# Two attention layers over 128 rows: a new order of the first layer's mixes, gated sum, turns and statistics

## The reference

```python
# layer 0: 8 heads of 32 channels, attention over the 256 tokens of a row
x = layernorm(x1d)                                  # over channels
q, k, v = split(x @ qkv_w.T)
aff = einsum('bmich,bmjch->bmijh', q, k)
gate = sigmoid(x @ gate_w.T + gate_b)
weights = softmax(aff + bias[:, None])              # bias = x2d @ x2d_w.T / sqrt(32)
out = (einsum('bmrch,bmirh->bmich', v, weights) * gate) @ final_w.T + final_b
# layer 1: 4 heads of 64 channels, |i - j| <= 16, no gate
```

## Time and profile before

| what | value |
|---|---|
| median of three runs | 3649.43 us |
| the profiled execution | 3664.15 us |
| its span, first to last instruction | 3662.3 us |
| mean granted clock of TensorE over the span | 0.969 of full speed |
| busy: PE, DVE, ACT, POOL | 92%, 82%, 76%, 59% |
| from 300 to 2200 us (layer 0): PE, DVE, ACT, POOL busy in 1900 us | 1788.69, 1685.45, 1680.21, 1496.18 us |
| granted clock from 300 to 2200 us | 1.00 |
| from 2400 to 3600 us (layer 1): PE, DVE, ACT, POOL busy in 1200 us | 1200.00, 969.89, 839.27, 493.42 us |

### The profile page before, as it was taken

The page is one execution under the profiler, slowest core; times in us unless marked ns, Lnnn a source line. Parts: engine busy times, 40 slices in busy tenths (PEclk is TensorE's granted clock), DMA queues, the critical chain, the costliest instruction groups (busy, mean ns, idle before and its releaser), DMA issues.

```text
span 3662.3 us, 122873 instructions
## 1 busy us (share of the span) xinstructions
PE 3372.3 (92%) x36747; PEld 3007.4 (82%) x36747; DVE 3002.9 (82%) x10850; ACT 2776.3 (76%) x8999; POOL 2177.9 (59%) x4107
## 2 busy tenths in 40 slices
PE   4459999999999999999999999799999999999999
PEld 1148888888888888888888888699999999999998
DVE  4458988888888888888888888688888888888887
ACT  1148888988888888888888988567667677776776
POOL 0047777777777777787777777444444444444443
PEclk7569999999999999999999999899999999999999
DMA  9921111111111111111111111011111111111111
GB/s 341 349 100 54 46 49 51 44 52 45 50 52 43 52 46 48 52 43 52 46 48 50 44 52 44 30 53 52 52 52 52 52 53 54 53 52 52 52 52 47
DMA packets 189032, 238.42 MB, mean 65 GB/s; under 512 B 11824, under 2 KB 176176, under 8 KB 184752
## 3 DMA queue, kind: packets, MB, share of 16 engines
q1 hardware_dynamic: 184368, 204.17, 17.7%
q10 hardware_dynamic: 4608, 33.56, 2.5%
HBM read 170.57 MB, written 67.11 MB: 65 GB/s over the span
## 4 chain that ended last, share of the span: by engine, by line
PE 58%; ACT 14%; issue 11%; DMA 6%; DVE 6%; POOL 2%; DVEq 1%; SPq 1%; ACTq 1%; POOLq 0%
PE work L477 24%; ACT prob L722 7%; PE work L486 7%; PE turn L527 5%; PE score L617 5%; PE mix L650 4%; DMA x_chunk<-xT 4%; PE mix L539 3%; PE score L505 3%; DMA x_tok<-x_nat 3%; PE turn L634 3%; ACT xnT L741 2%; ACT probT L728 2%; PE turn L635 2%; PE turn L636 2%
## 5 line engine op out<-in xcount | busy, mean ns | idle before, releaser
L364 POOL TENSOR_SCALAR prob<-prob,row_inv 128x256 f32<-128x256 f32 x2048 | 1068.0, 540 | 206.1 <-DVE row_inv L932 204.9
L722 ACT ACTIVATE prob<-prob,row_min 128x256 f32<-128x256 f32 x2048 | 1028.1, 507 | 128.3 <-DVE row_min L926 123.6
L477 PE MATMUL work<-src,w 128*128 128x256 f32 x7680 | 1067.5, 288 | 10.4 <-DVE src L915 6.7
L477 PEld LDWEIGHTS work<-src,w 128*128 128x128 f32 x7680 | 951.0, 189 | 12.3 <-DVE src L915 7.4
L415 POOL TENSOR_SCALAR prob<-prob,row_inv 128x160 f32<-128x160 f32 x1024 | 391.0, 401 | 767.4 <-DVE row_inv L1042 767.4
L926 DVE CUSTOM_DVE_ANT_0 prob<-score,neg_bias 128x256 f32<-128x256 f32 x2048 | 749.5, 417 | 17.2 <-PE score L505 10.1
L527 PE MATMUL turn<-ident,prob 128*128 128x128 f32 x3072 | 484.8, 280 | 120.0 <-ACT probT L728 101.4
L789 ACT ACTIVATE prob<-prob,row_min 128x160 f32<-128x160 f32 x1024 | 431.4, 426 | 141.7 <-DVE row_min L1035 141.6
L527 PEld LDWEIGHTS turn<-ident,prob 128*128 128x128 f32 x3072 | 336.3, 141 | 233.2 <-ACT probT L728 125.6
L477 PE MATMUL work<-att,wf 128*128 128x256 f32 x3072 | 432.1, 290 | 4.4 <-DVE att L981 3.0
L486 PE MATMUL work<-w,src 128*128 128x256 f32 x3072 | 425.8, 288 | 0.0
(11 more groups left out here) (110 smaller groups left out, 6225.7 us busy)
## 6 DMA issues: line engine op xcount, KB each, us to landing
pair_chunk<-pairT ACTq DMA_DIRECT2D x32, 1024.0 KB, 8.0
x_chunk<-xT SPq DMA_DIRECT2D x32, 1024.0 KB, 8.5
x_tok<-x_nat SPq DMA_DIRECT2D x128, 256.0 KB, 3.3
x_sb<-xT SPq DMA_DIRECT2D x128, 256.0 KB, 3.4
x1T<-y_sb SPq DMA_DIRECT2D x128, 256.0 KB, 2.2
x_sb<-x1T SPq DMA_DIRECT2D x128, 256.0 KB, 2.9
outT<-y_sb SPq DMA_DIRECT2D x128, 256.0 KB, 2.2
prob<-w_d SPq DMA_DIRECT2D x1, 1024.0 KB, 8.2
```

The lines of the kernel that those rows point to most:

```text
L364: pool.tensor_scalar(prob[:, h, ib], prob[:, h, ib], row_inv[:, h, ib:ib + 1], 1.0, ALU.mult, ALU.mult).then_inc(norm_done[0], 1)
L477: ins = pe.matmul(out[:, cb], w[:, of_w, kb, cols + cb * P:cols + (cb + 1) * P], x[:, of_x, kb], start=n == 0, stop=n == len(terms) - 1)
L722: act.activation(prob[:, h, ib], prob[:, h, ib], ACT.Exp, bias=row_min[:, h, ib:ib + 1], scale=-1.0, accum_out=row_sum[:, h, ib:ib + 1]).t ...
```

## The change

All of it lies in layer 0. Four engines' lists are rewritten; the same work is done.

- PE: the mixes of m-1 go ahead of `scores(m, 1)`. Turns 1, 3 and 6 go to the score bank in place of 3 and 7. Turn 6 stands ahead of the y projection. Turn 1 now waits for the minimum of head 4, which frees the bank, and no longer for ACT's copy of turn 0.
- ACT: k's high part goes between xnT and src's high part, exps 5 between the copy of turn 0 and xnT, exps 6 and 7 ahead of att's high part, the copy of turn 4 ahead of it too, and the copy of turn 6 ahead of exps 0 of the next row.
- DVE: att_sum goes ahead of minima 4 to 7; the copy of turn 1 goes between minima 6 and 7; att's low part behind minima 0 and 1 of the next row; the layer norm's statistics ahead of minima 2 and 3. The two instructions of gstat are now in two rows (`out_stats`): one ahead of the copy of turn 3 in odd iterations, one at the head of even iterations; the last of all stands behind the loop.
- POOL: ln_rstd, ln_off and xn stand ahead of `norms(nxt, 0)`, not behind it.
- SP: the load of x_tok stands ahead of the store and the load of x_sb; it waits only for POOL's scaling a row earlier.

The core of the diff:

```diff
@@ SP, rows @@
+                    if n == 0 and ahead.exists:
+                        wait(sp, gn_scaled, ahead.times(1, -1))
...
                     if last.exists:
                         wait(sp, y_done[n], m.times(1 if n == 0 else CB))
@@ PE, scores and turns @@
-                    wait(pe, turn_done[0][1], r.times(PAIRS0, 2 * hg - 2))
+                    if hg == 0:
+                        wait(pe, turn_done[0][1], r.times(PAIRS0, -2))
+                    else:
+                        wait(pe, turn_done[0][0], r.times(PAIRS0, 0))
...
-                    if h % HPG == HPG - 1:
+                    if h in (1, 3, 6):
                         to = score[:, 0].rearrange("p b t -> p (b t)")
...
+                    elif h == 1:
+                        wait(pe, min_done[0], m.times(TB * H0, TB * (HPG + 1)))
...
+                    elif h == 6:
+                        wait(pe, turn_done[0][1], m.times(PAIRS0, 2))
+                        if nxt.exists:
                             wait(pe, min_done[0], nxt.times(TB * H0, TB))
@@ PE, body0 @@
-                if m.exists:
-                    scores(m, 1)
                 if last.exists:
                     mixes(last, 0)
                     mixes(last, 1)
+                if m.exists:
+                    scores(m, 1)
...
                     turns(5)
+                    turns(6)
                 if last.exists:
                     wait(pe, att_done[0], last.times(1, 1))
@@ DVE, body0 @@
+                def out_stats(ob, r, pair):
+                    wait(dve, y_done[0], r.times(1, 1))
+                    apart(dve, dve_passed)
+                    at = slice(pair, pair + 1) if isinstance(pair, int) else bass.ds(pair, 1)
+                    dve.bn_stats(gstat1[:, ob, at], y_sb[:, ob].rearrange("p r t -> p (r t)")).then_inc(y_stats, 1)
...
+                    if done.base % 2 == 0 and (done + -1).exists:
+                        out_stats(1, done + -1, done.times(1, -1, of=2))
...
+                if done.exists and done.base % 2 == 1:
+                    out_stats(0, done, done.times(1, 0, of=2))
```

More of the change, by code:

```diff
@@ L735, in body0 @@
                     exps(m, 4)
-                    turn_copy(0)
+                    turn_copy(0, turn[:])
+                    exps(m, 5)
                 if far.exists:
@@ L743, in body0 @@
                                        ).then_inc(xnT_done, 1)
+                if nxt.exists:
+                    wait(act, k_ps[0], nxt.times(1, 1))
+                    act.copy(kT[:, nxt.base % 2, HIGH], work[:, 0]).then_inc(k_high[0], 1)
+                if far.exists:
                     wait(act, xnT_done, far.times(CB, CB))
@@ L747, in body0 @@
                 if m.exists:
[L748 to L753, removed]
+                    turn_copy(2, turn[:])
+                    exps(m, 6)
+                    exps(m, 7)
+                    turn_copy(4, turn[:])
                 if last.exists:
@@ L974, in body0 @@
                                       kT[:, nxt.base % 2, HIGH].bitcast(F32), ALU.subtract).then_inc(k_done[0], 1)
-                if m.exists:
-                    turn_copy(3, score[:, 0].rearrange("p b t -> p (b t)"))
                 if far.exists:
                     split_low(0, far, xnT[:])
-                if last.exists:
-                    wait(dve, att_high[0], last.times(1, 1))
-                    dve.tensor_tensor(att[:, LOW], att_sum[:], att[:, HIGH].bitcast(F32), ALU.subtract
-                                      ).then_inc(att_done[0], 1)
                 if nxt.exists:
@@ L988, in body0 @@
                     mins(nxt, 1)
-                    mins(nxt, 2)
-                if m.exists:
-                    turn_copy(5, turn[:])
-                if nxt.exists:
-                    mins(nxt, 3)
-                if nxt.exists:
-                    inverse(nxt, 0)
+                if last.exists:
+                    wait(dve, att_high[0], last.times(1, 1))
+                    dve.tensor_tensor(att[:, LOW], att_sum[:], att[:, HIGH].bitcast(F32), ALU.subtract
+                                      ).then_inc(att_done[0], 1)
                 if ahead.exists:
@@ L1002, in body0 @@
                 if m.exists:
-                    turn_copy(7, score[:, 0].rearrange("p b t -> p (b t)"))
+                    turn_copy(5, turn[:])
                 if ahead.exists:
@@ L1011, in body0 @@
                     dve.tensor_scalar(ln_var[:], ln_mv[:, :, 1], EPS, None, ALU.add).then_inc(ln_var_done, 1)
-                if done.exists and done.base % 2 == 1:
-                    wait(dve, y_done[0], done.times(1, 1))
-                    apart(dve, dve_passed)
-                    for ob in range(CB):
-                        pair = done.base // 2
-                        at = slice(pair, pair + 1) if done.loop is None else bass.ds(done.times(1, 0, of=2), 1)
-                        dve.bn_stats(gstat1[:, ob, at], y_sb[:, ob].rearrange("p r t -> p (r t)")).then_inc(y_stats, 1)
+                if nxt.exists:
+                    mins(nxt, 2)
+                    mins(nxt, 3)
+                    inverse(nxt, 0)
+                if m.exists:
+                    turn_copy(7, turn[:])
             over_rows(dve, 3, 2, body0)
+            dve.wait_ge(y_done[0], ROWS)
+            dve.bn_stats(gstat1[:, 1, ROWS // 2 - 1:ROWS // 2], y_sb[:, 1].rearrange("p r t -> p (r t)")).then_inc(y_stats, 1)
             dve.wait_ge(y_stats, CB * ROWS // 2)
```

86 lines of the change are left out of this document (40 added, 46 removed).

## The result

| | median, us | lowest to highest | executions |
|---|---|---|---|
| before | 3653.14 | 3649.16 to 3661.97 | 4 |
| changed | 3620.63 | 3619.16 to 3621.66 | 4 |

The changed kernel takes 0.9907 of the time of before (95% interval 0.9887 to 0.9928), about 34 us less. Forecast were 3624 us and faster.

What follows compares the result with a forecast made beforehand. Layer 0's row time was taken as the bound, a chain of waits between engines with none busy throughout: 16.15 us a row against 16.35, 26 us over 128 rows, 3649.4 - 26 = 3624 us, range 3590 to 3668.

Steps and rivals of the forecast that it cites:

- The chain of seven steps: Layer 0, one row from scores(m, 1) to the next: 16.05 us, 16.15 in odd iterations, mean 16.10.
- step 3: Exps 5 (0.99), then xnT (1.02) on ACT; the v projection starts 0.06 after xnT, at 5.22 us.
- step 7: End of the row on PE: y 1.51, turn 7 0.41, q 1.59, mixes 1.87, sum 5.38 us.
- the 0.05 for unseen waits: Allowance in us added to the mean row of 16.10, giving 16.15 us a row.
- Rival A's first form: Att low holds head 6's second POOL multiply, turn 6 goes late: 16.49 a row, 3667 us; A 0.22 in all.
- The margin of 0.05 us: POOL's second multiply for head 6 starts at 9.59, ahead of att low at 9.64.
- rival B: Att low falls between POOL's multiplies, y waits only for turn 6: 15.88 a row, 3589 us; chance 0.15.
- step 6: DVE's att low meets POOL's multiply, is held and ends at 10.61; y starts at 10.67.
- A's second form: POOL over 0.5 us late, head 6's first multiply caught too: 17.00 a row, 3733 us; chance 0.13.
- Moved at no price: X_tok's load ahead on SP's queue, and POOL's xn and norms 0 changing places, were costed at nothing.
- the prediction's room of 0.8 us: DVE's spare time up to head 4's minimum in even iterations, said to cover the statistics half at the head.
- Rival C: Stalls only change names, PE waiting for head 4's minimum, then xnT: row stays 16.35, 3649 us; chance 0.15.

Runs made afterwards that it cites:

- 2: The changed kernel with both statistics instructions together again at the iteration's end: 0.9922 of before, 5 us more than the change.
- 4: The changed kernel with att's low part reading the mixes in PSUM, not att_sum in SBUF, gate left out of it, so output differs: 0.9849 of before.
- 7: The changed kernel with the gated sum written over the mixes in PSUM and both parts of att read from there: 3601.17 us, 0.9844 of before.
- 1: The kernel before with only the statistics split over two rows, at the change's places: 1.0061 of before, 22 us slower.
- 6: The kernel before with only turns 1, 3 and 6 put in the score bank, with the needed waits and copies: 0.9988 of before, 4 us less.

## Why the prediction was right, and where it wasn't

**The chain of seven steps held.** Up to y no step is off by more than 0.09 us, and v starts when xnT is there, as step 3 has it. Its sum gave 0.20 a row less; 0.26 was measured. That the time came within 4 us is in part luck: rows without a held multiply are 0.22 shorter than the 16.15 forecast, one row in four has what was left to a rival, which gives 0.16 of it back in the mean, and the median of before is 3.7 us above the one that the 26 us were taken from.

**The last leg and the allowance were the sizes that were off.** In step 7 y, turn 7, q and the mixes take 5.30, not 5.38, and the 0.05 for unseen waits wasn't needed; undisturbed rows are 15.85 to 16.10, not 16.05 to 16.15. (The last statistics stand behind the loop only in the change, not "as before"; no sum uses that.)

**Rival A's first form is part of the truth.** I forecast one row for all and gave A 0.22. The margin of 0.05 us was lost in one row in four: 0.07 to 0.15 in the three, 0.00 in the fourth. It comes with the split of the statistics, since 2 has no such row; how the split moves att low in just this one wasn't followed. So the mean of 16.09 is that of a chain shorter than mine, (15.88 + 16.03 + 15.89) / 3 = 15.93, and of a meeting lost in every fourth row, 16.59 (A laid it at 16.49). Where att low can't be caught nor catch, in 4 and 7, rows take 15.92 in the mean, 15.8 to 16.0, near the 15.88 that rival B laid for that: what 7 saves is the fourth row. In the other three att low is held for 0.2, but turn 6 stands ahead of y, and PE comes to turn 6 without a wait only at 10.19. Y starts 0.46 behind it in place of 0.41 (1009.39 - 1008.98): the hold that step 6 made the end of the chain costs them 0.05, not the 0.17 by which B priced it.

**A's second form is real and is kept off by x_tok's load.** "Moved at no price" was right of the change and wrong of the step. Taken out, the load's place costs 71 us and POOL's order 83. The load shortens POOL's chain enough for head 6's multiplies; the prediction called it hidden work. That it is "worth at most what POOL holds up PE" was so, but in the new order this was 72.0 us from 300 to 2200 us, up to 1.1 in a row.

**The statistics were read too simply.** The long row was put down to them. They do make it: split in the old order, the alternation falls from 1.42 to 0.39 (1). But the kernel is slower for it, so the gain isn't there. In the new order one piece costs 0.3 in every second row (2), where the prediction's room of 0.8 us would leave 0.5, and the split that saves it brings the row of 16.59. Most of the alternation went with the rest of the order, from 1.42 to 0.3 with the piece still whole. How much of it the mixes ahead of the scores bring, how much the gated sum ahead of the minima and how much turn 6 ahead of y, was not tried one by one.

**Rival C happened to half of the change.** Banks alone only rename the wait (6). In the full change the wait at turn 1 is for minima and small (35.1 us in 118 rows).

**The rule on the port.** In the ordinary row att low starts 0.60 behind POOL's first multiply (1018.19), so within the second, and is held for its rest: 0.87 in place of 0.69. The Trainium skill (SBUF — State Buffer, "SBUF: two separate sides") says that the port pair that VectorE (DVE) and GpSimd (POOL) share is held for the whole instruction by whoever starts first, and that a DVE instruction takes it with two SBUF inputs; the trace agrees, and so does experiment 7, where att low has one input in PSUM and takes 692 ns in 113 rows of 113. That rule kept A's first form away only with the 0.05 in POOL's favour. In 29 rows there was no margin: att low came 0.84 behind the inverse, just when POOL's second multiply was due (0.38 + 0.46), and both start at 1002.28.

## What to carry to other kernels

Where an order is written by hand for several engines, its steps have no price of their own: price them within the new order, and ask of each "free" step what it would cost if it alone were missing. Read the rows also where the sum is unchanged: in experiment 2 two effects of 0.6 us in four rows hid behind a difference of 5 us in the time. Follow to the end of its queue every wait that one moves across. Where two engines keep meeting on an SBUF operand at a margin of hundredths of a microsecond, don't time the meeting: take it away, here by leaving one operand in PSUM, which gave 23 us more for four edited lines.

## What the runs showed of the hardware

Who holds whom at nearly equal starts isn't told by the order of starts in the trace. In the earlier trace rows POOL started 0.05 ahead and was the one held, for 1.00. In another row of before POOL's second multiply started as far ahead (757.21 + 0.46 = 757.67), and src's low part was held:

```profile
757.21 0.94 POOL L364 TENSOR_SCALAR prob<-prob,row_inv 128x256 f32<-128x256 f32 x2
...
757.72 0.97 DVE L915 TENSOR_TENSOR src<-xnT,src 128x512 fp32r<-128x512 f32 x1
```

In the changed kernel, from 300 to 2200 us, the starts lie within 0.02 us of each other in 88 cases. Src's low part was the one held in all 59 of its cases (1.01 to 1.02 long), and POOL's multiply in all 29 with att's low part (0.98).

A DVE instruction that is held ends 0.54 behind the end of POOL's, though it takes 0.68 where it isn't held, so it loses 0.14 less than if it had started only then; here too (757.72 + 0.97 = 758.69, 757.21 + 0.94 = 758.15). And the busy time of PE misleads: between 300 and 2200 us it rose from 1788.69 to 1851.38, 3.5%, for 1.6% more instructions of the same kinds. The ends of matmuls are modelled, so the rest is not to be read as work.
